# A fused decoder layer: the rounds of scores in the cross-attention stage are set apart, each between halves or thirds of full-height products

## The chip, the cores and the metric

One NeuronCore of a Trainium2 chip runs the whole program in one launch. The metric is the device time of one execution in microseconds (us). The engines named below are TensorE (PE, with its weight loads shown as PEld), VectorE (DVE), ScalarE (ACT), GpSimd (POOL) and the DMA queue of SyncE (SP). Each runs its own list of instructions in order, and waits on semaphores.

## The reference

Input x is 4 x 1024 x 512 in fp32, the context 4 x 2048 x 384. Three sublayers follow each other, each with a residual and a layer norm: linear attention, a cross sublayer, and a feed-forward with quantized weights and activations. Only the cross sublayer matters here. Cut to that:

```
Q = (x_text @ Wq).reshape(Bb, Tt, H, DH)                 # H = 4 heads, DH = 32
scores = einsum('bthd,bghd->bhtg', Q, K) / sqrt(DH)      # 2048 keys
topv, topi = top_k(scores, 32)
probs = softmax(topv)
attn_mean = zeros.at[..., topi].set(probs).mean(axis=1)
c_t = attn_mean @ V
x = layernorm(x_text) * (1 + gate * scale_in(c_t)) + gate * shift_in(c_t)
y = s4d(x)                                               # a long convolution, by FFT
y = y * (1 + gate * scale_out(c_t)) + gate * shift_out(c_t)
h = gelu(layernorm(x_text + y) @ W1 + b1) @ W2 + b2
```

## The kernel before, in words

The program runs its stages one after the other: `a_` (linear attention), `p_` (preparation of keys, film weights and convolution kernel), `c_` (cross, the function `cross`), and `f_` (feed-forward). The change is in `cross` alone.

`cross` works in 32 tiles of 128 tokens (`t`), eight per batch element, with four heads each; head number `j = 4 t + h`. The work of a head goes through all engines:
- PE makes the scores: `queries(t)` turns the tile x (transposes) and projects q. `scores(t, p)` makes those of the head pair `p`: four rounds of 512 keys, each round one product of 32 rows for each of the two heads, and one of a single row that adds the mask. The result lies in PSUM, `p_s`, with one bank per head of the pair, so that a round waits for ACT to have copied the last one.
- ACT copies the scores to SBUF (`copy_s`, the ring `s` of five rows).
- DVE finds the top 32 of 2048 in four scans (MAX8 and MATCH_REPLACE8, lines 1490 to 1498). In the middle of a head's scans stands the reciprocal of the previous head's softmax sum (`invert`, line 1483).
- ACT's `below(j)` marks what is under the 32nd value and sums the exponentials; POOL's `cut(j)` subtracts the marks; ACT's `weigh(j)` takes the exponential, and `diagonal(j)` makes a diagonal of the reciprocal.
- PE's `attn(j)` multiplies the weights by this diagonal and so turns them: 16 products of 128 x 128 (the turning products), summed over four heads in `p_a`. `copy_a` moves them to SBUF.

Once per tile PE makes `context` (48 products with the values), `film` in two parts (twice two accumulations of 512 columns), and what belongs to the convolution: `spectra` (the forward products, 64 columns each) and `slot` (tiles 0 to 7 transpose the convolution's kernel, tiles 11 and on make the inverse products). `context`, `film`, `queries`, `spectra` and `slot` share the two PSUM banks `p_m`, so each waits for ACT to copy the one before it (`copy_q`, `copy_f`, `copy_u`, `copy_slot`, `copy_fi`, `copy_fo`). POOL makes the convolution's small transforms: `transform` behind `copy_f`, from tile 10 on also `convolved` and `finished`, between the cuts; and `modulate` applies the first film part and stores the tile.

The order on each engine is written out by hand, as one loop over tiles per engine; nothing reorders it. In a step `t` of that loop PE does `attn` of the last two heads of tile t-1 and the first two of tile t, the scores of pair 1 of tile t in one block of four rounds, and those of pair 0 of tile t+1 in another. SP loads x, the normalized x, keys and values of the next batch, and spectra, in its own loop with its waits.

One product in fp32 is two instructions on PE, so 16 turning products are 32 in the trace, and 48 are 96. The names `c_p_s`, `c_p_a`, `c_p_m`, `c_s` in the profile are the tiles `p_s`, `p_a`, `p_m`, `s` of the code.

Of the kernel before, what the change touches and what calls it, by code (L numbers as in the profile page):

```python
# [8 lines left out]
ACT = mybir.ActivationFunctionType  # L9
# [5 lines left out]
P = 128  # L15
B, S, D = 4, 1024, 512
TOK = B * S
CH = S // P
# [436 lines left out]
N2, DV, NH2 = 2048, 384, 4  # L455
# [433 lines left out]
def cross(nc, x1, xn, keysT, values, film_w, film_b, mask_row, text_mask, Wq, eye, xm, mod_out, conv_k, D_skip, dft, idft,  # L889
# [4 lines left out]
    with ExitStack() as ctx:  # L894
# [106 lines left out]
        def forwards(t):  # L1001
            return sum(forward_job(i) is not None for i in range(t + 1))
# [142 lines left out]
        def _(pe):  # L1145
# [1 line left out]
            pe.wait_ge(core_in, 16 * 3)  # L1147
            pe.wait_ge(consts, 2)

            def queries(t):  # L1150
# [4 lines left out]
                last.then_inc(xT_done, 1)  # L1155
                pe.wait_ge(xT_copied, t + 1)
                for k in range(KD):
                    last = mm(p_m[:, 1, 0:P], wq[:, k, :], xT[:, k * P:(k + 1) * P], start=(k == 0), stop=(k == KD - 1))
                last.then_inc(q_done, 1)

            def scores(t, p):
                pe.wait_ge(q_copied, t + 1)
                pe.wait_ge(keys_in, 80 * (t // CH + 1))
                for c in range(4):
                    cols = slice(c * 512, (c + 1) * 512)
                    for i in range(2):
                        r = HS * (2 * p + i)
                        at_least(pe, s_copied, (t * 2 + p) * 8 + 2 * c + i - 1)
                        mm(p_s[:, i, :], qT[r:r + HS, t % 2, :], kt[r:r + HS, cols], start=True, stop=False)  # L1169
                        mm(p_s[:, i, :], oneb[r:r + 1, :], mrow[r:r + 1, cols], start=False, stop=True).then_inc(s_done, 1)  # L1170

            def attn(j):
                t, h = j // NH2, j % NH2
                if h == 0:
                    at_least(pe, aT_copied, t)
                pe.wait_ge(diag_ready, j + 1)
                pe.wait_ge(w_ready, j + 1)
                for n in range(GB):
                    last = mm(p_a[:, n, :], s[:, j % RING, n * P:(n + 1) * P], diag[:, j % 2, :],  # L1179
                              start=(h == 0 and n % 4 == 0), stop=(h == NH2 - 1 and n % 4 == 3),  # L1180
                              skip_group_check=True)
                last.then_inc(attn_done, 1)

            def spectra(t):

# [37 lines left out]
            def context(t):  # L1223
                at_least(pe, f_copied, forwards(t + 1))
                pe.wait_ge(values_in, 16 * (t // CH + 1))
                pe.wait_ge(aT_copied, t + 1)
                if t + 2 < TILES:
                    pe.wait_ge(xT_copied, t + 3)
                for k in range(KV3):
                    for n in range(GB):  # L1230
                        last = mm(p_m[:, 0, k * P:(k + 1) * P], vals[:, n, k * P:(k + 1) * P], aT[:, n, :],  # L1231
                                  start=(k == 0 and n == 0), stop=(k == KV3 - 1 and n == GB - 1),
                                  skip_group_check=True)
                last.then_inc(uT_done, 1)

            def film(t, part):
                if part == 0:
# [12 lines left out]
                    last = mm(p_m[:, n, :], oneb[0:BR, :], fb[:, c * D:(c + 1) * D], start=False, stop=True)  # L1250
                last.then_inc(fo_done if part else fi_done, 1)

            queries(0)
            scores(0, 0)
# [23 lines left out]
            attn(LAST - 1)  # L1278
            attn(LAST)
            slot(TILES)  # L1280
            context(TILES - 1)
            film(TILES - 1, 0)

            def rest_forward(i):
# [34 lines left out]
        def _(act):  # L1319
            a = nc.scalar.activation  # L1320

            def copy_q(t):
                act.wait_ge(xT_done, t + 1)
                at_least(act, q_done, t)
                a(xT[:], p_m[:, 0, :], ACT.Copy).then_inc(xT_copied, 1)
                act.wait_ge(q_done, t + 1)
                a(qT[:, t % 2, :], p_m[:, 1, 0:P], ACT.Copy).then_inc(q_copied, 1)

            def copy_s(t, p, part):
                at_least(act, attn_done, (t - 1) * NH2 + 2 * p + 1)  # L1330
                for c in range(2 * part, 2 * part + 2):
                    for i in range(2):
                        act.wait_ge(s_done, (t * 2 + p) * 8 + 2 * c + i + 1)
                        a(s[:, (t * NH2 + 2 * p + i) % RING, c * 512:(c + 1) * 512], p_s[:, i, :], ACT.Copy).then_inc(s_copied, 1)  # L1334

            def below(j):

# [52 lines left out]
            def copy_slot(t):  # L1390
# [5 lines left out]
                else:  # L1396
                    at_least(act, y_out, 16 * (g - NCB))
                    a(yb[:].rearrange("p n c -> p (n c)"), p_m[:, 1, :], ACT.Copy).then_inc(slot_copied, 1)  # L1398

            copy_q(0)  # L1400
            copy_s(0, 0, 0)
            copy_s(0, 0, 1)
            for t in range(TILES):
                j = t * NH2
                if t:
                    below(j - 1)
                if t > 1:
                    copy_fo(t - 2)
                copy_s(t, 1, 0)
                if t:  # L1410
                    weigh(j - 1)
                    diagonal(j - 1)
                copy_s(t, 1, 1)
                if t + 1 < TILES:
                    copy_q(t + 1)
# [6 lines left out]
                weigh(j)  # L1422
                diagonal(j)

                below(j + 1)
                if t:
                    copy_u(t - 1)
                if t + 1 < TILES:
                    copy_s(t + 1, 0, 0)
                weigh(j + 1)  # L1430
                diagonal(j + 1)
                if t + 1 < TILES:
                    copy_s(t + 1, 0, 1)
                if slot_job(t) is not None:
                    copy_slot(t)

                below(j + 2)
                if t:
                    copy_fi(t - 1)
                weigh(j + 2)  # L1440
                diagonal(j + 2)
            below(LAST)
            weigh(LAST)
            diagonal(LAST)
            copy_fo(TILES - 2)
# [101 lines left out]
        def _(pool):  # L1547
# [69 lines left out]
            for t in range(TILES):  # L1617
                job = forward_job(t)
                masked_identity(t)
                j = t * NH2  # L1620
                if t:
                    cut(j - 1)
                if t > 1:
                    store_mod(t - 2)
# [7 lines left out]
                if t:  # L1632
# [5 lines left out]
            cut(LAST)  # L1638
            store_mod(TILES - 2)
            modulate(TILES - 1)  # L1640
            store_mod(TILES - 1)
# [770 lines left out]
```

## Time and profile before

| | us |
|---|---|
| three runs | 5045.29, 5044.64, 5043.18 |
| median | 5044.64 |
| profiled execution | 5042.79 |
| its span | 5040.9 |
| PE busy | 4416.3 (88%) |
| DVE busy | 3805.5 (75%) |
| POOL busy | 2186.9 (43%) |
| ACT busy | 2068.8 (41%) |

The span is the time from the first to the last instruction of the profiled execution; 1.9 us lie around it. The cross stage is from about 978 us (the first scan of DVE) to some 3530 us. "Busy" of PE counts pipelined matmuls with modelled ends. PEclk is TensorE's granted clock, 1.00 for 2.4 GHz and 0.50 for 1.2 GHz. In the page's 40 slices it reads 9 and more in the first stages, and 7 to 8 in the cross stage.

### The profile page before, as it was taken

The numbers are of one execution on the slowest core, as the hardware profiler recorded it, in microseconds if no ns is written. First come the engines' busy times: TensorE is split into PE (matmuls) and PEld (weight loads), VectorE is DVE, ScalarE is ACT, GpSimd is POOL, SyncE is SP. The second block draws the span as 40 slices with busy tenths as digits, with TensorE's granted clock in tenths as the row PEclk, the third lists the DMA queues.
The fourth block names the chain that finished last, engine by engine and source line by source line (L and its number), as shares of the span: only waits on it lengthen the run. The fifth ranks groups of instructions, "written<-read, shape, count | busy, mean of one in ns | idle before, by whom it ended". The sixth has DMA issues, their size and how long they took to land. (4 is left out here: it accounts for less than half of the span.)

```text
span 5040.9 us, 70529 instructions
## 1 busy us (share of the span) xinstructions
PE 4416.3 (88%) x28066; PEld 3194.9 (63%) x28066; DVE 3805.5 (75%) x4097; ACT 2068.8 (41%) x3816; POOL 2186.9 (43%) x2260
## 2 busy tenths in 40 slices
PE   8999977589999999999999999987579989898984
PEld 6777753356665676676766667667456666666662
DVE  5666659699999988888788887876256767777667
ACT  3433322144444444444444444431234545444453
POOL 1111116435454566766667666670233333333321
PEclk9999988678888877777777777788789999999996
DMA  2111115300011001111011110023531211111101
GB/s 84 51 46 50 49 48 185 118 24 28 24 42 61 26 28 34 38 53 36 28 32 38 54 37 26 30 69 76 193 104 43 61 44 58 47 58 54 51 26 36
DMA packets 214587, 275.98 MB, mean 55 GB/s; under 512 B 96659, under 2 KB 144403, under 8 KB 210224
## 3 DMA queue, kind: packets, MB, share of 16 engines
q1 hardware_dynamic: 196850, 216.91, 14.2%
q0 software_dynamic: 17408, 54.56, 2.9%
q8 instruction: 222, 3.64, 0.3%
q14 instruction: 107, 0.88, 0.1%
HBM read 186.44 MB, written 84.98 MB: 54 GB/s over the span
## 5 line engine op out<-in xcount | busy, mean ns | idle before, releaser
L1555 POOL TENSOR_TENSOR c_s<-c_s,c_z 128x2048 f32<-128x2048 f32 x128 | 580.5, 4535 | 792.8 <-ACT c_z L1344 790.8
L1875 PE MATMUL f_p_g<-f_hT,f_w 128*128 128x128 f32 x4096 | 538.3, 295 | 69.8 <-ACT f_gT L1975 55.4
L1496 DVE MAX8 c_top<-c_z 128x8 f32<-128x2048 f32 x256 | 585.0, 2285 | 4.7 <-issue 0.2
L1875 PEld LDWEIGHTS f_p_g<-f_hT,f_w 128*128 128x128 f32 x4096 | 526.7, 211 | 90.4 <-ACT f_gT L1975 58.2
L1497 DVE MATCH_REPLACE8 c_z<-c_top,c_z 128x2048 f32<-128x2048 f32 x256 | 582.6, 2276 | 0.0
L1169 PE MATMUL c_p_s<-c_kt,c_qT 32*128 32x512 f32 x1024 | 500.9, 864 | 87.1 <-ACT c_s L1334 85.8
L1179 PEld LDWEIGHTS c_p_a<-c_diag,c_s 128*128 128x128 f32 x4096 | 528.2, 211 | 49.5 <-ACT c_diag L1358 25.8
L1179 PE MATMUL c_p_a<-c_diag,c_s 128*128 128x128 f32 x4096 | 531.3, 293 | 25.2 <-ACT c_diag L1358 25.2
L1883 PE MATMUL f_p_o<-f_w,f_gT 128*128 128x512 f32 x1024 | 481.8, 592 | 0.0
L1334 ACT ACTIVATE c_s<-c_p_s 128x512 f32<-128x512 f32 x512 | 278.2, 594 | 455.0 <-PE c_p_s L1170 454.6
L1249 PE MATMUL c_p_m<-c_wf,c_uT 128*128 128x512 f32 x768 | 415.7, 684 | 22.6 <-ACT c_yb L1398 16.3
L1231 PE MATMUL c_p_m<-c_aT,c_vals 128*128 128x128 f32 x3072 | 393.3, 296 | 38.1 <-ACT c_fz L1388 33.4
L1231 PEld LDWEIGHTS c_p_m<-c_aT,c_vals 128*128 128x128 f32 x3072 | 387.3, 211 | 42.5 <-ACT c_fz L1388 37.5
L1169 PEld LDWEIGHTS c_p_s<-c_kt,c_qT 32*128 32x128 f32 x1024 | 173.7, 233 | 294.7 <-ACT c_s L1334 283.9
L1249 PEld LDWEIGHTS c_p_m<-c_wf,c_uT 128*128 128x128 f32 x768 | 164.4, 222 | 213.8 <-issue 211.7
L1498 DVE MAX8 c_top<-c_z 128x8 f32<-128x2048 f32 x128 | 293.8, 2295 | 4.4
L1490 DVE MAX8 c_top<-c_s 128x8 f32<-128x2048 f32 x128 | 293.8, 2295 | 4.4
L1491 DVE MATCH_REPLACE8 c_z<-c_top,c_s 128x2048 f32<-128x2048 f32 x128 | 291.3, 2276 | 0.0
L2124 DVE TENSOR_TENSOR f_hs<-f_p_c,f_rs 128x257 f32<-128x257 f32 (+1 forms) x256 | 108.6, 424 | 232.1 <-PE f_p_c L1894 230.6
L1352 ACT ACTIVATE c_s<-c_s,c_nb 128x2048 f32<-128x2048 f32 x128 | 255.2, 1994 | 27.9 <-POOL c_s L1555 27.9
L1344 ACT ACTIVATE c_z<-c_s,c_tb 128x2048 f32<-128x2048 f32 x128 | 256.3, 2002 | 0.0
L1883 PEld LDWEIGHTS f_p_o<-f_w,f_gT 128*128 128x128 f32 x1024 | 174.5, 190 | 123.8 <-issue 115.8
(362 smaller groups left out, 8103.4 us busy)
## 6 DMA issues: line engine op xcount, KB each, us to landing
mod_out<-c_fo POOLq DMA_DIRECT2D x32, 512.0 KB, 3.0
f_mr<-mod_out SPq DMA_DIRECT2D x32, 512.0 KB, 4.8
p_ct<-in_ctxT SPq DMA_DIRECT2D x16, 768.0 KB, 5.1
c_vals<-in_ctx SPq DMA_DIRECT2D x4, 3072.0 KB, 12.0
c_kb<-kspec SPq DMA_DIRECT2D x22, 512.0 KB, 3.3
a_xt<-in_xT SPq DMA_DIRECT2D x32, 256.0 KB, 3.1
a_xr<-in_x SPq DMA_DIRECT2D x32, 256.0 KB, 2.6
x<-a_out POOLq DMA_DIRECT2D x32, 256.0 KB, 2.5
```

The costliest lines, as they stand in the source:

```text
L1169: mm(p_s[:, i, :], qT[r:r + HS, t % 2, :], kt[r:r + HS, cols], start=True, stop=False)
L1179: last = mm(p_a[:, n, :], s[:, j % RING, n * P:(n + 1) * P], diag[:, j % 2, :], start=(h == 0 and n % 4 == 0), stop=(h == NH2 - 1 and n % ...
L1231: last = mm(p_m[:, 0, k * P:(k + 1) * P], vals[:, n, k * P:(k + 1) * P], aT[:, n, :], start=(k == 0 and n == 0), stop=(k == KV3 - 1 and n ...
L1249: mm(p_m[:, n, :], uT[:, k, :], wf[:, k, c * D:(c + 1) * D], start=(k == 0), stop=False)
L1490: st.link(v.max(best[0], row))
L1491: st.link(v.match_replace(work, best[0], row, NEG))
L1496: st.link(v.max(best[n], work))
L1497: st.link(v.match_replace(work, best[n], work, NEG))
L1498: v.max(best[3], work).then_inc(z_done, 1)
L1555: pool.tensor_tensor(row, row, low, ALU.subtract).then_inc(cut_ready, 1)
L1875: last = mm(p_g[:, f % 8, :], w1[:, k, f * P:(f + 1) * P], hT[:, k * P:(k + 1) * P], start=(k == 0 and f % 4 == 0), stop=(k == KD - 1 and ...
L1883: last = mm(p_o[:], gT[:, f, :], w2[:, f, :], start=(f == 0), stop=(f == FT - 1))
```

## The change

`scores` makes one round per call, `queries` is divided in `turn` (transposes) and `queries` (projection), `attn` in two halves of 8 products, `context` in its three accumulations. PE's loop then puts single rounds between them. The second part of `film` moves to the next step, and with it `copy_fi`, `copy_fo` and POOL's `modulate`. ACT's loop copies one round at a time, on both sides of `weigh` and `diagonal`, and copies the slot's result behind `weigh` of the third head. The instructions themselves are as they were; after the last tile the two halves of `attn` and one part of `film` follow.

```diff
-            def scores(t, p):
+            def scores(t, p, c):
                 pe.wait_ge(q_copied, t + 1)
                 pe.wait_ge(keys_in, 80 * (t // CH + 1))
-                for c in range(4):
-                    cols = slice(c * 512, (c + 1) * 512)
-                    for i in range(2):
+                cols = slice(c * 512, (c + 1) * 512)
+                for i in range(2):
...
-            def attn(j):
+            def attn(j, part):
                 t, h = j // NH2, j % NH2
-                if h == 0:
-                    at_least(pe, aT_copied, t)
-                pe.wait_ge(diag_ready, j + 1)
-                pe.wait_ge(w_ready, j + 1)
-                for n in range(GB):
+                if part == 0:
+                    if h == 0:
+                        at_least(pe, aT_copied, t)
+                    pe.wait_ge(diag_ready, j + 1)
+                    pe.wait_ge(w_ready, j + 1)
+                for n in range(8 * part, 8 * part + 8):
...
                 if t:
-                    attn(j - 2)
-                scores(t, 1)
+                    attn(j - 2, 0)
+                scores(t, 1, 0)
+                if t:
+                    attn(j - 2, 1)
+                if t > 1:
+                    film(t - 2, 1)
+                scores(t, 1, 1)
+                if t + 1 < TILES:
+                    turn(t + 1)
+
+                if t:
+                    attn(j - 1, 0)
+                scores(t, 1, 2)
+                if t:
+                    attn(j - 1, 1)
                 if t + 1 < TILES:
                     queries(t + 1)
-                if t:
-                    attn(j - 1)
                 if forward_job(t) is not None:
                     spectra(t)
+                scores(t, 1, 3)
                 if t:
-                    context(t - 1)
-                attn(j)
+                    context(t - 1, 0)
+
+                attn(j, 0)
                 if t + 1 < TILES:
-                    scores(t + 1, 0)
+                    scores(t + 1, 0, 0)
+                attn(j, 1)
+                if t:
+                    context(t - 1, 1)
+                if t + 1 < TILES:
+                    scores(t + 1, 0, 1)
+                if t:
+                    context(t - 1, 2)
+
+                attn(j + 1, 0)
+                if t + 1 < TILES:
+                    scores(t + 1, 0, 2)
+                attn(j + 1, 1)
                 if slot_job(t) is not None:
                     slot(t)
+                if t + 1 < TILES:
+                    scores(t + 1, 0, 3)
                 if t:
                     film(t - 1, 0)
-                attn(j + 1)
-                if t:
-                    film(t - 1, 1)
...
                 below(j)
                 if t:
                     copy_a(t - 1)
+                copy_s(t, 1, 2)
+                if t + 1 < TILES:
+                    copy_q(t + 1)
+                weigh(j)
+                diagonal(j)
                 if forward_job(t) is not None:
                     copy_f(t)
...
             for t in range(TILES):
                 job = forward_job(t)
                 if t:
                     cut(j - 1)
                 if t > 1:
+                    modulate(t - 2)
+                cut(j)
+                if t > 1:
                     store_mod(t - 2)
-                cut(j)
...
                 cut(j + 2)
-                if t:
-                    modulate(t - 1)
```

PE in a step from tile 11 on, before: from the end of the block for pair 1 (1154 transposes, 1158 q, 1179 turning products, 1199 forward products, 1231 context) to the start of the next block.

```order
L1154 MATMUL c_p_m<-c_ident,c_xt 128x128 x4
L1158 MATMUL c_p_m<-c_xT,c_wq 128x128 x4
L1179 MATMUL c_p_a<-c_diag,c_s 128x128 x16
L1199 MATMUL c_p_m<-c_cx,c_fm 128x64 x16
L1231 MATMUL c_p_m<-c_aT,c_vals 128x128 x48
L1179 MATMUL c_p_a<-c_diag,c_s 128x128 x16
L1169 MATMUL c_p_s<-c_kt,c_qT 128x512
L1170 MATMUL c_p_s<-c_mrow,c_oneb 128x512
```

The same place in the changed kernel (1181 turning products, 1170 and 1171 a round, 1160 q, 1202 forward products):

```order
L1154 MATMUL c_p_m<-c_ident,c_xt 128x128 x4
L1181 MATMUL c_p_a<-c_diag,c_s 128x128 x8
L1170 MATMUL c_p_s<-c_kt,c_qT 128x512
L1171 MATMUL c_p_s<-c_mrow,c_oneb 128x512
L1170 MATMUL c_p_s<-c_kt,c_qT 128x512
L1171 MATMUL c_p_s<-c_mrow,c_oneb 128x512
L1181 MATMUL c_p_a<-c_diag,c_s 128x128 x8
L1160 MATMUL c_p_m<-c_xT,c_wq 128x128 x4
L1202 MATMUL c_p_m<-c_cx,c_fm 128x64 x16
L1170 MATMUL c_p_s<-c_kt,c_qT 128x512
```

The projection of q moved behind a head's turning products, and a round stands inside these; the next round stands behind the forward products.

ACT around the copy of the slot product, before (1334 scores, 1398 slot copy, 1340 to 1346 `below(j+2)`, 1373 copy_fi, 1352 `weigh`, 1358 `diagonal`):

```order
L1334 ACTIVATE c_s<-c_p_s 128x512 x4
L1398 ACTIVATE c_yb<-c_p_m 128x512
L1340 ACTIVATE c_tb<-c_top 128x1
L1341 ACTIVATE c_nb<-c_top 128x1
L1344 ACTIVATE c_z<-c_s,c_tb 128x2048
L1346 ACTIVATE c_topx,c_den<-c_top,c_nb 128x32
L1373 ACTIVATE c_fi<-c_p_m 128x1024
L1352 ACTIVATE c_s<-c_s,c_nb 128x2048
L1358 ACTIVATE c_diag<-c_identm,c_rd 128x128
```

The same head in the changed kernel (1376 to 1382 `below`, 1370 scores, 1388 `weigh`, 1434 slot copy, 1394 `diagonal`):

```order
L1376 ACTIVATE c_tb<-c_top 128x1
L1377 ACTIVATE c_nb<-c_top 128x1
L1380 ACTIVATE c_z<-c_s,c_tb 128x2048
L1382 ACTIVATE c_topx,c_den<-c_top,c_nb 128x32
L1370 ACTIVATE c_s<-c_p_s 128x512 x2
L1388 ACTIVATE c_s<-c_s,c_nb 128x2048
L1434 ACTIVATE c_yb<-c_p_m 128x512
L1394 ACTIVATE c_diag<-c_identm,c_rd 128x128
L1370 ACTIVATE c_s<-c_p_s 128x512 x2
```

The slot copy moved from ahead of `below` to behind `weigh` of the same head, and copy_fi left this head.

## Rows read from the trace of the kernel before

**Rows 1.** List of waits, whole span: engine, line, released by: us in total, times, longest.

```profile
DVE c_rd L1483 <- issue: 282.0, 54, 10.6
```

**Rows 2.** DVE in order of time: start, us, line, instruction, idle time before it.

```profile
1110.62 2.29 DVE L1490 MAX8 c_top<-c_s 128x8 f32<-128x2048 f32 x1
...
1744.70 2.29 DVE L1490 MAX8 c_top<-c_s 128x8 f32<-128x2048 f32 x1
...
2404.93 2.29 DVE L1490 MAX8 c_top<-c_s 128x8 f32<-128x2048 f32 x1
...
2421.47 2.29 DVE L1490 MAX8 c_top<-c_s 128x8 f32<-128x2048 f32 x1
...
2441.39 0.16 DVE L1483 RECIPROCAL c_rd<-c_den 128x1 f32<-128x1 f32 x1 [10.52 <-issue]
...
2448.49 2.29 DVE L1490 MAX8 c_top<-c_s 128x8 f32<-128x2048 f32 x1
...
2476.33 0.16 DVE L1483 RECIPROCAL c_rd<-c_den 128x1 f32<-128x1 f32 x1 [1.89 <-issue]
```

**Rows 3.** Windows: stretch, us, busy of PE, PEld, DVE, ACT, POOL, granted clock, DMA.

```profile
2400.26:2478.77 78.51, 73.58 (x379) 54.07 (x377) 65.21 (x45) 33.91 (x53) 52.00 (x60) 0.78 0.10 31
2421.70:2425.60 3.90, 2.97 (x12) 1.00 (x9) 3.87 (x3) 2.25 (x5) 3.90 (x2) 1.00 0.00 0
2425.80:2442.60 16.80, 15.80 (x48) 10.07 (x46) 6.21 (x6) 6.98 (x12) 9.52 (x11) 0.50 0.15 47
2480.40:2483.60 3.20, 2.09 (x19) 1.95 (x19) 3.13 (x3) 1.56 (x3) 0.38 (x2) 1.00 0.00 0
```

**Rows 4.** PE in order of time, one step from tile 11 on.

```profile
2400.06 3.68 PE L1199 MATMUL c_p_m<-c_cx,c_fm 128*128 128x64 f32 x32
2404.86 12.61 PE L1231 MATMUL c_p_m<-c_aT,c_vals 128*128 128x128 f32 x96 [1.11 <-ACT c_fz L1388]
2417.31 3.74 PE L1179 MATMUL c_p_a<-c_diag,c_s 128*128 128x128 f32 x32
2420.97 1.13 PE L1169 MATMUL c_p_s<-c_kt,c_qT 32*128 32x512 f32 x4
...
2423.06 1.18 PE L1169 MATMUL c_p_s<-c_kt,c_qT 32*128 32x512 f32 x3 [0.73 <-ACT c_s L1334]
...
2431.15 7.09 PE L1219 MATMUL c_p_m<-c_fv,c_gm 128*128 128x64 f32 x32
2439.01 4.66 PE L1249 MATMUL c_p_m<-c_wf,c_uT 128*128 128x512 f32 x6 [0.78 <-ACT c_yb L1398]
...
2450.09 2.74 PE L1249 MATMUL c_p_m<-c_wf,c_uT 128*128 128x512 f32 x6
```

**Rows 5.** ACT in order of time, the same step.

```profile
2400.26 1.88 ACT L1363 ACTIVATE c_aT<-c_p_a 128x2048 f32<-128x2048 f32 x1 [2.53 <-PE c_p_a L1179]
2403.78 1.02 ACT L1388 ACTIVATE c_fz<-c_p_m 128x1024 f32<-128x1024 f32 x1 [1.64 <-PE c_p_m L1199]
...
2425.41 1.99 ACT L1352 ACTIVATE c_s<-c_s,c_nb 128x2048 f32<-128x2048 f32 x1
...
2427.60 1.07 ACT L1334 ACTIVATE c_s<-c_p_s 128x512 f32<-128x512 f32 x2
...
2438.27 0.60 ACT L1398 ACTIVATE c_yb<-c_p_m 128x512 f32<-128x512 f32 x1 [6.42 <-PE c_p_m L1219]
...
2438.99 2.00 ACT L1344 ACTIVATE c_z<-c_s,c_tb 128x2048 f32<-128x2048 f32 x1
```

**Rows 6.** POOL in order of time: transform, cut, first and last of convolution.

```profile
2404.88 1.28 POOL L827 TENSOR_TENSOR c_fw<-c_fz 128x512 f32<-128x512 f32 x1 [2.82 <-ACT c_fz L1388]
...
2416.53 4.55 POOL L1555 TENSOR_TENSOR c_s<-c_s,c_z 128x2048 f32<-128x2048 f32 x1
2421.03 2.37 POOL L1601 TENSOR_TENSOR c_fz<-c_fw,c_kb 128x1024 f32<-128x1024 f32 x1
...
2433.33 0.73 POOL L864 TENSOR_TENSOR c_ft<-c_fz 128x256 f32<-128x256 f32 x1
```

More of the change, by code:

```diff
@@ L1148, in _, with turn @@
             pe.wait_ge(consts, 2)
-            def queries(t):
+            def turn(t):
                 pe.wait_ge(x_in[t % 2], 16 * (t // 2 + 1))
@@ L1155, in queries @@
                 last.then_inc(xT_done, 1)
+            def queries(t):
                 pe.wait_ge(xT_copied, t + 1)
@@ L1181, in attn @@
                               skip_group_check=True)
-                last.then_inc(attn_done, 1)
+                if part:
+                    last.then_inc(attn_done, 1)
             def spectra(t):
@@ L1221, in slot, with context @@
                 last.then_inc(slot_done, 1)
[L1223 to L1234, printed above, removed]
+            def context(t, k):
+                if k == 0:
+                    at_least(pe, f_copied, forwards(t + 1))
+                    pe.wait_ge(values_in, 16 * (t // CH + 1))
+                    pe.wait_ge(aT_copied, t + 1)
+                    if t + 2 < TILES:
+                        pe.wait_ge(xT_copied, t + 3)
+                for n in range(GB):
+                    last = mm(p_m[:, 0, k * P:(k + 1) * P], vals[:, n, k * P:(k + 1) * P], aT[:, n, :],
+                              start=(k == 0 and n == 0), stop=(k == KV3 - 1 and n == GB - 1),
+                              skip_group_check=True)
+                if k == KV3 - 1:
+                    last.then_inc(uT_done, 1)
             def film(t, part):
@@ L1251, in film @@
                 last.then_inc(fo_done if part else fi_done, 1)
+            turn(0)
             queries(0)
-            scores(0, 0)
+            for c in range(4):
+                scores(0, 0, c)
             for t in range(TILES):
@@ L1320, in _, with copy_x @@
             a = nc.scalar.activation
-            def copy_q(t):
+            def copy_x(t):
                 act.wait_ge(xT_done, t + 1)
@@ L1325, in copy_q, with copy_s @@
                 a(xT[:], p_m[:, 0, :], ACT.Copy).then_inc(xT_copied, 1)
+            def copy_q(t):
                 act.wait_ge(q_done, t + 1)
                 a(qT[:, t % 2, :], p_m[:, 1, 0:P], ACT.Copy).then_inc(q_copied, 1)
-            def copy_s(t, p, part):
+            def copy_s(t, p, c):
                 at_least(act, attn_done, (t - 1) * NH2 + 2 * p + 1)
[L1331 to L1334, printed above, removed]
+                for i in range(2):
+                    act.wait_ge(s_done, (t * 2 + p) * 8 + 2 * c + i + 1)
+                    a(s[:, (t * NH2 + 2 * p + i) % RING, c * 512:(c + 1) * 512], p_s[:, i, :], ACT.Copy).then_inc(s_copied, 1)
             def below(j):
@@ L1398, in copy_slot @@
                     a(yb[:].rearrange("p n c -> p (n c)"), p_m[:, 1, :], ACT.Copy).then_inc(slot_copied, 1)
+            copy_x(0)
             copy_q(0)
-            copy_s(0, 0, 0)
-            copy_s(0, 0, 1)
+            for c in range(4):
+                copy_s(0, 0, c)
             for t in range(TILES):
@@ L1407, in _ @@
                 if t > 1:
-                    copy_fo(t - 2)
+                    copy_fi(t - 2)
                 copy_s(t, 1, 0)
@@ L1412, in _ @@
                     diagonal(j - 1)
+                if t > 1:
+                    copy_fo(t - 2)
                 copy_s(t, 1, 1)
                 if t + 1 < TILES:
-                    copy_q(t + 1)
+                    copy_x(t + 1)
                 below(j)
@@ L1419, in _ @@
                     copy_a(t - 1)
+                copy_s(t, 1, 2)
[3 more added lines that the diff above has]
+                diagonal(j)
                 if forward_job(t) is not None:
                     copy_f(t)
-                weigh(j)
-                diagonal(j)
+                copy_s(t, 1, 3)
                 below(j + 1)
-                if t:
-                    copy_u(t - 1)
                 if t + 1 < TILES:
@@ L1433, in _ @@
                     copy_s(t + 1, 0, 1)
+                if t:
+                    copy_u(t - 1)
+                below(j + 2)
+                if t + 1 < TILES:
+                    copy_s(t + 1, 0, 2)
+                weigh(j + 2)
                 if slot_job(t) is not None:
                     copy_slot(t)
[L1437 to L1440, printed above, removed]
                 diagonal(j + 2)
+                if t + 1 < TILES:
+                    copy_s(t + 1, 0, 3)
             below(LAST)
+            copy_fi(TILES - 2)
             weigh(LAST)
@@ L1631, in _ @@
                 cut(j + 2)
-                if t:
-                    modulate(t - 1)
                 if job is not None and not of_kernel(job):
@@ L1638, in _ @@
             cut(LAST)
+            modulate(TILES - 2)
             store_mod(TILES - 2)
```

19 lines of the change are left out of this document (12 added, 7 removed).

## Prediction, made before the changed kernel was run

> **What bounds the kernel now.** I read the list of waits first, for the engine with the steadiest work in the cross stage: VectorE (DVE), which scans four heads per tile. It is to be seen there that its idle time in the stage is one entry, 282.0 us in 54 waits ahead of the reciprocal c_rd [rows 1]. Then DVE's rows in order of time, for where these waits stand. An undisturbed head takes 16.54 us, from 2404.93 to 2421.47, so a tile cannot take less than 66.2 us. In a late tile the head that begins at 2421.47 has a wait of 10.52 us in its middle, and two heads later there is one of 1.89 us [rows 2]; 66.2 + 12.4 = 78.6, and from one copy of p_a to the same copy a tile later it is 78.51 us [rows 3]. The nine tiles from 1110.62 to 1744.70 took 634.1 us, 38.6 more than 9 x 66.16 [rows 2]. The remaining 282 - 39 = 243 us lie in the 20 tiles after them, the last of 32 apart. These two numbers, 39 and 243, are all that an order of work can give back.
>
> Why the 10.52 us? The reciprocal waits for the sum that ScalarE (ACT) makes in `below`. Head j+2 was scanned at 2421.47, but `below(j+2)` has its large instruction at 2438.99, because ACT stood 6.42 us at copy_slot ahead of it [rows 5], which waits for TensorE's (PE's) slot product, which stands behind four rounds of scores [rows 4]. So PE is late, and what makes it late is its clock as much as its work. PE is busy 73.58 us of a tile at a mean granted clock of 0.78 [rows 3]. As only 1.0 and 0.5 (2.4 and 1.2 GHz) appear, it was at half for (1 - 0.78) x 2 x 78.51 = 34.5 us, which cost 17 us of work: at full rate PE would be busy for some 57 us, less than DVE's 66.2.
>
> What precedes a fall is in the windows. From 2421.7 to 2425.6 PE did only score products (32 rows high), 2.97 us busy of 3.90, at full clock; the next 16.80 us are at half. Another fall is short: the end of the 64-column forward products and a wait, 2.09 us busy of 3.20 at full, half behind it [rows 3]. Eight rounds per tile in two blocks of four are thus where most of the half-clock time comes from (the block, and the slot product and half a film behind it). A round costs 1.36 us at full clock (2420.97 to 2423.06 less the wait of 0.73), and in a block PE then waits for ACT's two copies of 1.07 us [rows 4, 5].
>
> **The change, part by part.** Each round now stands between products of full height: a head's turning products (3.74 us) are cut in two halves around a round, context in thirds. The instructions are the same; no DMA is added. PE gains two things: the copies of a round run beside other products (each round's period of about 2.0 us falls to 1.36: 8 x 0.65, less where it waited at half clock, about 4 us), and between a round and the next there are at least 1.9 us of full-height work, so that the block that preceded the fall is gone. I take the clock as full there. No row shows such a mixture; the nearest, half a tile of pure products, is at full clock, and pure rounds lose it, so the bounds are "full everywhere" and "half everywhere".
>
> What the change adds is coupling. ACT copies the slot result only behind `weigh(j+2)`, and the first film product waits for that copy; the film's second half moves a slot later, behind copy_fi; the forward products wait for q_copied, now behind copy_a and a copied round. POOL has its transform and its convolution between the cuts as before, but now `cut(j+2)` holds the film. That closes a loop over one tile, and I add it up. T is when DVE starts a tile's first head, directly after ACT's last copy of its scores; the slot copy is 1.6 us before T (what ACT does behind it: diagonal and the round, from the rows weigh to copy, 2.2 - 1.9 + 1.1, with handoffs).
> - film, first half: two accumulations of 2.74 us, 5.6 at full. PE has been idle before it (below), so it begins at half clock as at 2439.01, where the first took 4.66: + 1.9. Ends T + 5.9.
> - turning product and one round 3.7 + 1.4; film, second half 5.6; a round and the transpose 2.0; turning product and a round 5.1: T + 23.7 [rows 4].
> - ACT: copy_a 1.88, a round 1.07, q 0.3: T + 27.0 [rows 5].
> - forward products 3.68 at full; 7.1 at half, as the slot product of the same shape took [rows 4]; copy_f 1.02: T + 31.7 or T + 35.1.
> - POOL: from 2404.88 transform, cut and convolution to 2434.06 are 29.2, and the next cut is 4.5: + 33.7 [rows 6]: T + 65.4 or T + 68.8.
> - ACT: weigh and diagonal 2.2, slot copy 0.5, round 1.1 [rows 5]: T + 69.2 or 72.6, and a dozen handoffs at 0.1 (copy_f ends at 2404.80, POOL starts at 2404.88): 70.4 or 73.8.
>
> So a late tile is bound by this loop, not by DVE. Between the two values I take 72.5: PE has 2.4 us without work ahead of the forward products (q projection over, q not yet copied), like the wait of 1.1 in front of context behind which the clock fell, and loses the clock somewhere in them. PE idles then 5 us or more ahead of the film. DVE will stand some 5 us at two heads' starts together, for c_s, not at c_rd.
>
> Late tiles: 243 - 20 x (72.5 - 66.2) = 117 us saved. Of the nine early tiles only the last has a convolution (and the one before it no forward job): without its 13 us POOL's loop has slack, and it counts whether the tile's second pair of heads has its scores in time. q is copied 5.8 us behind a head's end (`below` 2.5, from the end of the copy at 2438.87 to DVE's start at 2441.39; copy_a 1.9; a round 1.1; q 0.3), forward products 3.7 to 7.1, a round 1.4 to 2.9, and the copies of both (2), in sum 12.9 to 17.8 against 16.5. I leave 0.5 us for each and 2 for the ninth, 6 of the 39 us: 33 saved. The first two tiles have no wait and keep none. Three times the keys of the next batch are loaded behind the last round of the old ones, and that round now stands closer to the first of the new: a context third (12.61 / 3 = 4.2) and half a product (1.9) are between, 6 us. No row here prices this; bounds are 0 and 4 us for each of three loads, I take 0. The film half that moves behind the last tile lies beside the last head's cut (ACT and POOL then take over 9 us): 0, bounds 0 and 3. Sum: 5042.8 - 150 = 4893 for the profiled execution; the median shown is 1.9 above it, so 4895.
>
> **The rule that speaks against it.** The Trainium skill, "TensorE: Matmul & The Clock Gate", section "Why this matters for your kernels", asks that there be no long idle gap between bursts of matmuls, since one returns the clock to half rate; it says nothing of matmuls that fill only a quarter of the array's rows. By it alone, the score blocks would not cost clock, and the new idle stretches of 2.4 and 5 us would: the sum would have no clock gain and come near the slower rival below. The trace bears out more than the rule: in front of the fall at 2425.8 PE had one wait of 0.73 us for a copy and was else at work [rows 3, 4].
>
> **Rivals.**
> - Smaller gain: forward products, the round behind them and the first context third all at half, a round more at half in the film's slot: 73.8 + 1.5 or so, 75.3 per late tile. 243 - 182 + 20 = 81 saved: 4964. For it: a 64-column product behind a wait already lost the clock once.
> - Larger gain: forward products and film keep the full clock: 70.4 - 1.9 = 68.5. 243 - 46 + 36 = 233 saved: 4812. Against it: the idle time ahead of both. The end of this side is DVE unhindered everywhere, 4763.
> - Slower: the loop's PE part (27 us at full) runs mostly at half clock, since PE now waits at three places in the loop and a round stands in each stretch. The loop reaches today's 78.5 when 12 us of work at half clock are added to those I took (they cost 6). With the first film wholly at half (3.7 more), the first turning product and round (5) and the second film (5.6) it is 72.5 + 14.3 = 86.8: 20 x 8 = 160 slower, and the early gain gone, 5205. Against it: in the rows the film regains the full clock before it ends (the second of its two accumulations, like that at 2450.09, takes 2.74).
> - No change: the late tile stays at 78.5 by another wait (a DMA of x or xn, now asked for one slot later). Nothing in the rows is near; 5044.
>
> **How the numbers follow.** Forecast (70.4 to 74 per late tile, 4860 to 4930) 0.45, smaller gain (up to 4990) 0.27, larger gain 0.13, none 0.04, slower 0.11. Faster by over 0.2% (about what a measurement of this kernel can tell from no change) 0.85, within it 0.04, slower 0.11. The range goes from the middle of the larger gain, 4825, to the end of the smaller, 4990.
>
> **What would show it.** Right: late tiles of 71 to 74 us with DVE's waits at c_s (the MAX8 on c_s) instead of c_rd; no half clock between turning products and rounds; mean granted clock of a tile near 0.85; PE idle over 4 us ahead of the first film product, released by c_yb's copy; POOL's gap between the convolution and the cut of head j+2 gone. Wrong: half clock across several halves of turning products, which means that one round is enough to lose it; POOL's cut not being late; or late tiles at 66 us, which breaks the loop.

## The result

| | before | changed |
|---|---|---|
| median, us (4 runs each) | 5044.97 | 4898.96 |
| lowest and highest | 5043.18, 5045.51 | 4896.70, 4902.59 |
| profiled execution, its span | 5042.79, 5040.9 | 4900.3, 4898.4 |

The ratio is 0.9712, 95% interval 0.9695 to 0.9729: 2.9% faster. The forecast was 4895 us, a ratio of 0.970.

### The profile page after: what moved, and what is told of

It is laid out like the page before. It is cut to its first block and busy times, and to the rows that moved or that the text cites. A ratio compares the mean times of both kernels' runs of the same rounds, so it can differ in the third digit from the quotient of the medians.

```text
span 4898.4 us, 70845 instructions
## 1 busy us (share of the span) xinstructions
PE 4201.7 (86%) x28066; PEld 3061.9 (63%) x28066; DVE 3798.7 (78%) x4097; ACT 2061.7 (42%) x3816; POOL 2187.6 (45%) x2260
## 5 line engine op out<-in xcount | busy, mean ns | idle before, releaser
L1923 PE MATMUL f_p_g<-f_hT,f_w 128*128 128x128 f32 x4096 | 539.4, 295 | 67.4 <-ACT f_gT L2023 53.0
L1181 PEld LDWEIGHTS c_p_a<-c_diag,c_s 128*128 128x128 f32 x4096 | 489.2, 195 | 119.0 <-issue 90.7
L1253 PE MATMUL c_p_m<-c_wf,c_uT 128*128 128x512 f32 x768 | 420.0, 690 | 142.2 <-ACT c_yb L1434 120.6
L1234 PEld LDWEIGHTS c_p_m<-c_aT,c_vals 128*128 128x128 f32 x3072 | 420.8, 224 | 61.7 <-issue 59.7
L1234 PE MATMUL c_p_m<-c_aT,c_vals 128*128 128x128 f32 x3072 | 435.1, 310 | 3.8 <-ACT c_aT L1399 2.5
L1537 DVE MAX8 c_top<-c_s 128x8 f32<-128x2048 f32 x128 | 293.8, 2295 | 139.2 <-ACT c_s L1370 136.4
L1170 PE MATMUL c_p_s<-c_kt,c_qT 32*128 32x512 f32 x1024 | 333.7, 720 | 20.1 <-ACT c_s L1370 19.8
L1202 PE MATMUL c_p_m<-c_cx,c_fm 128*128 128x64 f32 x960 | 185.2, 383 | 70.5 <-ACT c_qT L1364 70.5
```

The source lines that it names most:

```text
L1253: mm(p_m[:, n, :], uT[:, k, :], wf[:, k, c * D:(c + 1) * D], start=(k == 0), stop=False)
L1537: st.link(v.max(best[0], row))
L1923: last = mm(p_g[:, f % 8, :], w1[:, k, f * P:(f + 1) * P], hT[:, k * P:(k + 1) * P], start=(k == 0 and f % 4 == 0), stop=(k == KD - 1 and ...
```

## The profile after

The waits of DVE first, in the list of waits of the changed kernel (us in total, times, longest). Line 1537 is the MAX8 on c_s, a head's first scan; 1253 is film, 1202 the forward products.

```profile
DVE c_top L1537 <- ACT c_s L1370: 136.4, 48, 5.8
PE c_p_m L1253 <- ACT c_yb L1434: 120.6, 21, 9.0
PE c_p_m L1202 <- ACT c_qT L1364: 70.5, 29, 4.5
```

The wait of film for the slot copy was there before, but short:

```profile
PE c_p_m L1249 <- ACT c_yb L1398: 16.3, 21, 0.8
```

The 282.0 us at c_rd [rows 1] are gone as an entry, and 136.4 us have come at the heads' starts: DVE now waits for scores. PE's wait for the slot copy has grown from 16.3 to 120.6 us, and its wait for q is new. Then DVE in order of time: the tile that starts at 1723.14 (tile 11) is the first of the 20 late ones, those in which the convolution's inverse products are made, and 2369.34, 2440.13 and 2513.72 are three tile starts in a row, to hold against [rows 2].

```profile
1112.46 2.29 DVE L1537 MAX8 c_top<-c_s 128x8 f32<-128x2048 f32 x1
...
1723.14 2.30 DVE L1537 MAX8 c_top<-c_s 128x8 f32<-128x2048 f32 x1 [1.43 <-ACT c_s L1370]
...
2369.34 2.29 DVE L1537 MAX8 c_top<-c_s 128x8 f32<-128x2048 f32 x1 [2.10 <-ACT c_s L1370]
...
2404.96 2.30 DVE L1537 MAX8 c_top<-c_s 128x8 f32<-128x2048 f32 x1 [2.57 <-ACT c_s L1370]
...
2440.13 2.29 DVE L1537 MAX8 c_top<-c_s 128x8 f32<-128x2048 f32 x1 [2.12 <-ACT c_s L1370]
...
2513.72 2.29 DVE L1537 MAX8 c_top<-c_s 128x8 f32<-128x2048 f32 x1 [2.09 <-ACT c_s L1370]
```

The nine early tiles take 610.7 us from 1112.46 to 1723.14, 15 over 9 x 66.16 (39 before). A late tile takes about 70.8 us (nine of the twenty) or 73.6 to 74.0 us (ten), not strictly in turn, and the mean over twenty is 72.1. The windows of two such tiles, and of two stretches inside (busy of PE, PEld, DVE, ACT, POOL, granted clock, DMA), answer to [rows 3]:

```profile
2369.34:2440.13 70.79, 63.29 (x377) 46.79 (x377) 65.21 (x44) 33.59 (x53) 51.98 (x60) 0.89 0.11 34
2440.13:2513.72 73.59, 65.20 (x377) 48.33 (x377) 65.21 (x44) 33.59 (x54) 51.96 (x60) 0.85 0.10 33
2378.00:2395.00 17.00, 16.28 (x92) 10.10 (x88) 16.76 (x12) 9.87 (x14) 5.58 (x4) 1.00 0.23 63
2468.70:2480.00 11.30, 11.30 (x48) 9.40 (x49) 5.87 (x3) 4.77 (x8) 3.89 (x6) 0.50 0.09 37
```

From 2378 to 2395 PE does turning products, three rounds, film, transposes and the projection, all at full clock. PE's idle time in a tile has not gone down: it was 4.9 us (78.51 less 73.58) and is now 7.5 and 8.4. What has gone down is its busy time for the same instructions, from 73.6 to 63.3 and 65.2 us. The stretch at half is the forward products, the round behind them and the start of context. PE in order of time shows where the two tiles differ, to hold against [rows 4]:

```profile
2368.13 4.69 PE L1253 MATMUL c_p_m<-c_wf,c_uT 128*128 128x512 f32 x6 [5.59 <-ACT c_yb L1434]
...
2378.83 2.05 PE L1181 MATMUL c_p_a<-c_diag,c_s 128*128 128x128 f32 x16
...
2393.22 1.06 PE L1160 MATMUL c_p_m<-c_xT,c_wq 128*128 128x128 f32 x8
2396.59 4.67 PE L1202 MATMUL c_p_m<-c_cx,c_fm 128*128 128x64 f32 x32 [2.31 <-ACT c_qT L1364]
...
2467.82 7.06 PE L1202 MATMUL c_p_m<-c_cx,c_fm 128*128 128x64 f32 x32 [2.31 <-ACT c_qT L1364]
```

The forward products take 4.67 us in one tile and 7.06 in the next: behind the wait of 2.31 us the clock falls in their midst or ahead of them, which is 2.4 of the 2.8 us between the two tiles. On ACT the slot copy, behind POOL's late cut and `weigh`, starts at 2438.20, 1.9 us ahead of the next tile's start. On POOL the gap between the convolution and this cut is gone, as forecast:

```profile
2430.93 0.73 POOL L864 TENSOR_TENSOR c_ft<-c_fz 128x256 f32<-128x256 f32 x1
2431.74 4.53 POOL L1602 TENSOR_TENSOR c_s<-c_s,c_z 128x2048 f32<-128x2048 f32 x1
```

## The experiments

All are compared with the kernel before on the same chip. "Late tile" is the mean distance of the starts of tiles 11 to 31 (before 78.4, changed 72.1), "early tile" that of tiles 2 to 11 (70.5 and 67.9), read from DVE's rows; DVE's own time is 66.2. In e4, e8 and e10 the scores are other numbers, since those products sum over all four heads; sizes and counts are the same.

| kernel | median us | ratio (95%) | early tile | late tile |
|---|---|---|---|---|
| e1 slot copy first | 4786.69 | 0.9478 (0.9463 to 0.9492) | 66.2 | 67.4 |
| e2 q copy first | 4801.04 | 0.9508 (0.9494 to 0.9523) | 66.2 | 68.1 |
| e3 both | 4755.63 | 0.9418 (0.9402 to 0.9433) | 66.2 | 66.2 |
| e4 before, full height | 4890.19 | 0.9684 (0.9670 to 0.9699) | 68.4 | 71.7 |
| e5 before, below first | 5068.15 | 1.0050 (1.0035 to 1.0065) | 72.7 | 78.0 |
| e6 whole turning products | 4805.95 | 0.9524 (0.9508 to 0.9539) | 66.3 | 68.3 |
| e7 rounds in pairs | 5038.82 | 0.9991 (0.9977 to 1.0005) | 70.6 | 77.5 |
| e8 changed, full height | 4983.69 | 0.9879 (0.9865 to 0.9894) | 70.8 | 74.8 |
| e9 whole and slot first | 4786.17 | 0.9478 (0.9464 to 0.9493) | 66.3 | 67.6 |
| e10 before, both edits | 4915.37 | 0.9732 (0.9715 to 0.9748) | 71.2 | 71.5 |

**Is it the height of the products that takes the clock?** e4 is the kernel before with one line changed.

```diff
-                        mm(p_s[:, i, :], qT[r:r + HS, t % 2, :], kt[r:r + HS, cols], start=True, stop=False)
+                        mm(p_s[:, i, :], qT[:, t % 2, :], kt[:, cols], start=True, stop=False)
```

> The kernel before, order untouched, with the score products over all 128 rows instead of the head's 32 (this sums over the four heads, so the scores are other numbers; sizes and counts are the same). It asks whether the height of the products or idle time takes PE's clock. A round takes 4 x 0.43 + 2 x 0.21 = 2.1 us at full clock instead of 1.36 and a wait of 0.66, so no time is gained by itself. Theory (the blocks of low products lose the clock): the two long half-clock stretches of a late tile go, the mean granted clock of a late tile goes from 0.78 to 0.95 or so, the tile from 78.5 to 66.2 to 69 us; 4780 to 4850. Rival (idle gaps alone lose it, height is nothing): clock 0.78 and 5040 to 5100, since the rounds no longer overlap.

The window of one late tile of e4, and the first round of a block, where the two heads no longer overlap:

```profile
2379.21:2450.39 71.18, 67.39 (x377) 44.78 (x376) 65.22 (x44) 34.57 (x52) 51.99 (x60) 1.00 0.11 34
```
```profile
2388.13 1.02 PE L1169 MATMUL c_p_s<-c_kt,c_qT 128*128 128x512 f32 x2
2389.08 0.39 PE L1170 MATMUL c_p_s<-c_mrow,c_oneb 1*128 1x512 bf16 x1
2389.40 1.12 PE L1169 MATMUL c_p_s<-c_kt,c_qT 128*128 128x512 f32 x2
2390.46 0.38 PE L1170 MATMUL c_p_s<-c_mrow,c_oneb 1*128 1x512 bf16 x1
2390.77 1.12 PE L1169 MATMUL c_p_s<-c_kt,c_qT 128*128 128x512 f32 x2
```

The clock is 1.00 over the whole tile, where it was 0.78 with the same order. From 1800 to 3100 us it is 0.99 in the mean, 0.78 before:

```profile
1800.00:3100.00 1300.00, 1231.76 (x6816) 821.35 (x6815) 1183.42 (x799) 628.12 (x944) 944.73 (x1075) 0.99 0.13 41
```
A round costs 2.6 us (2388.13 to 2390.77), twice as much as with low products, and the tile is still 7 us shorter. The longer rounds also fill most of the waits for the copies, so two things changed at once. In the kernel before, PE was busy for 15.80 of 16.80 us, mostly in low and 64-column products, and stayed at half all the same [rows 3], so it is not idle time that kept it there. What let it fall is not parted by this run: it can be the height of the products or the short waits between them (0.73 and 0.20 us ahead of the fall), and low rounds in a row without a wait were not run. The time is above my 4780 to 4850, since I had summed a round as 2.1 us: PE is busy for 67.4 of 71.2 us, which leaves little room for waits.

**Is it enough that ACT is unblocked?** e5 moves one call in the kernel before.

```diff
-                if slot_job(t) is not None:
-                    copy_slot(t)
-
                 below(j + 2)
+                if slot_job(t) is not None:
+                    copy_slot(t)
```

> The kernel before, with one move on ACT: below(j+2) ahead of the copy of the slot product, so that DVE's reciprocal, which had the 10.52 us wait, no longer waits behind PE's slot product. Theory (PE with its half-clock stretches is what bounds a late tile: 73.6 us busy and 5 waiting): the wait moves to another place of DVE, the late tile stays at 77 to 78.5, 5015 to 5050. Rival (the gain of the change is this unblocking of ACT, not the clock or the rounds): late tiles at 68 to 72, 4830 to 4910.

```profile
2390.73:2469.23 78.50, 73.56 (x377) 54.08 (x376) 65.21 (x44) 33.92 (x52) 52.03 (x59) 0.78 0.10 31
```

The same clock, the same PE time, the same 78.5. DVE's 12.4 us of waits in a tile (10.52 and 1.89) are 12.4 us again, ahead of the reciprocals of three heads:

```profile
2401.69 0.16 DVE L1483 RECIPROCAL c_rd<-c_den 128x1 f32<-128x1 f32 x1 [1.56 <-issue]
2425.58 0.17 DVE L1483 RECIPROCAL c_rd<-c_den 128x1 f32<-128x1 f32 x1 [7.38 <-issue]
2462.13 0.16 DVE L1483 RECIPROCAL c_rd<-c_den 128x1 f32<-128x1 f32 x1 [3.50 <-issue]
```

The kernel is 0.5% slower, outside my 5015 to 5050, mostly because the early tiles went from 70.5 to 72.7. The wait that the profile named was not the one to remove. e10 adds e5's edit to e4, to see whether ACT's order counts once the clock is full.

> The kernel before with both edits: score products over all 128 rows (other scores, same sizes) and below(j+2) ahead of the slot copy. Alone, the first took a late tile from 78.5 to 71.2 us with a DVE wait of 5 us at the reciprocal left, the second left it at 78.5. Theory (half clock bounds first, ACT's order second): together 66.2 to 68 us per late tile, 4760 to 4810. Rival (the 5 us are PE's work, since the full-height rounds are longer, and only change their place): 70 to 71.5, 4870 to 4900.

The rival was right on the tile: 71.5 us per late tile. The time, 4915, is above its range and 25 us above e4, as the early tiles went from 68.4 to 71.2. At full clock, too, this swap on ACT gives nothing; PE is busy for 66.4 of 70.0 us from 2350 to 2420, at a clock of 0.98.

**How many rounds may stand together?** e7 puts the changed kernel's rounds in pairs, e6 leaves them single but no longer cuts a head's turning products. Shown is one of the four places of each, on PE.

```diff
# e7
                     scores(t + 1, 0, 2)
+                    scores(t + 1, 0, 3)
                 attn(j + 1, 1)
# e6
                 attn(j, 0)
+                attn(j, 1)
                 if t + 1 < TILES:
                     scores(t + 1, 0, 0)
-                attn(j, 1)
```

> The changed kernel with the rounds in four pairs instead of eight single ones (two behind the turning products of heads j-2 and j, two between the halves of heads j-1 and j+1), their copies on ACT in pairs as well. PE then waits 0.66 us inside each pair, 2.6 us per tile. Theory (the clock falls behind a stretch of low products, and two rounds with the wait between are 3.4 us of it, about what stood ahead of the fall in the kernel before): some pairs lose the clock, the mean granted clock of a late tile falls below the changed kernel's 0.85 to 0.89, and late tiles take 75 to 79 us: 4955 to 5040. Rival (only blocks of four lose it): the waits alone, late tiles 72 to 74: 4900 to 4935.

> The changed kernel with a head's turning products in one piece: each single round stands behind the 16 products instead of between two halves of 8. Theory (it is enough that rounds stand singly): no fall of the clock is added, the late tiles stay at 70.7 to 73.7, 4885 to 4915. Rival (the halves matter, since without them a round stands next to a copy wait, a transpose or the forward products): half clock behind some rounds and late tiles of 75 us or more, 4950 and up.

e7 gives all of the gain back, as forecast (77.5 us per late tile, 5039). PE at one of its pairs:

```profile
2395.49 1.13 PE L1170 MATMUL c_p_s<-c_kt,c_qT 32*128 32x512 f32 x4
2396.45 0.39 PE L1171 MATMUL c_p_s<-c_mrow,c_oneb 1*128 1x512 bf16 x2
2397.66 1.52 PE L1170 MATMUL c_p_s<-c_kt,c_qT 32*128 32x512 f32 x4 [0.83 <-ACT c_s L1367]
2398.59 0.80 PE L1171 MATMUL c_p_s<-c_mrow,c_oneb 1*128 1x512 bf16 x2
2399.33 3.67 PE L1181 MATMUL c_p_a<-c_diag,c_s 128*128 128x128 f32 x16
```

The second round ends slower (0.80 instead of 0.39) and the eight turning products behind it take 3.67 us instead of 1.95: the clock fell in the pair. This is the rule and not one case: of the eight turning products that stand directly behind a round, from 1120 to 3160 us and where the trace has all their records, 110 of 111 take 2.05 us in the changed kernel, and 46 of 51 take 3.4 to 3.8 us in e7, where they stand behind a pair. Here are three tiles of e7, and an idle stretch of PE ahead of film in the changed kernel:

```profile
2360.04:2438.85 78.81, 71.07 (x374) 50.99 (x374) 65.22 (x45) 34.36 (x52) 50.36 (x59) 0.82 0.10 31
2438.85:2517.53 78.68, 68.45 (x377) 48.57 (x377) 65.20 (x44) 34.27 (x52) 51.88 (x60) 0.87 0.10 31
2206.38:2282.25 75.87, 65.88 (x365) 48.09 (x364) 65.21 (x44) 34.25 (x52) 51.56 (x60) 0.87 0.13 41
```
```profile
2362.60:2368.10 5.50, 0.00 (x0) 0.00 (x0) 4.60 (x3) 2.60 (x3) 5.41 (x8) 0.73 0.00 0
```

The mean clock of 0.82 to 0.87 is hardly less than the 0.85 and 0.89 above. But in the changed kernel part of the half clock lies where PE is idle, while in e7 more of it falls on work: PE is busy for 68.5 us in the mean of these three tiles instead of 64.2. The wait of 0.83 us in each pair is 3.3 us per tile beside that, and part of the loss.

e6 missed both forecasts: it is faster than the changed kernel by 93 us (4805.95 against 4898.96). PE at the place of the wait for q:

```profile
2276.51 3.74 PE L1181 MATMUL c_p_a<-c_diag,c_s 128*128 128x128 f32 x32
2280.17 1.13 PE L1170 MATMUL c_p_s<-c_kt,c_qT 32*128 32x512 f32 x4
2281.14 0.39 PE L1171 MATMUL c_p_s<-c_mrow,c_oneb 1*128 1x512 bf16 x2
2281.45 1.16 PE L1160 MATMUL c_p_m<-c_xT,c_wq 128*128 128x128 f32 x8
2283.45 3.76 PE L1202 MATMUL c_p_m<-c_cx,c_fm 128*128 128x64 f32 x32 [0.84 <-ACT c_qT L1362]
```

With whole products `p_a` is complete one round (1.4 us) earlier, so ACT copies it beside the round. The wait for q falls from 2.31 to 0.84, and the forward products keep the full clock (3.76). That is 1.5 us of wait and 0.9 to 3.3 of half clock (3.76 against 4.67 and 7.06), all of it in the loop: 68.3 instead of 72.1. The halves bought no clock; they cost 3.8 us a tile.

**Does a single round cost clock?** e8 is e4's line in the changed kernel.

> The changed kernel with score products over all 128 rows (they sum over the four heads, so the scores are other numbers). A round takes 2.7 us at full clock instead of 1.36 and no longer overlaps its two heads, as the rounds of the full-height run of the kernel before show. Theory (a single round between full-height products costs no clock, what is left of half clock comes from PE's two waits): the mean clock of a late tile rises only because PE has less to wait, and no more than 3 us of half clock go; five rounds of the loop cost 1.4 each, late tiles 76 to 80 and 4980 to 5060, slower than the changed kernel. Rival (single rounds still cost clock): the time stays or falls, 4850 to 4900, at a clock of 0.95 and more.

```profile
2348.46:2426.43 77.97, 75.66 (x377) 49.98 (x377) 65.21 (x45) 34.24 (x54) 51.36 (x58) 0.88 0.10 31
2426.43:2498.62 72.19, 67.30 (x377) 44.92 (x376) 65.21 (x45) 34.08 (x54) 52.45 (x62) 0.99 0.10 33
```

The kernel is 1.7% slower than the changed one, and 4984 is in the range of the theory; the late tile, 74.8 us in the mean, is below its 76 to 80. The wait for q is 2.31 us in every late tile. Behind it the forward products take 7.06 us in one tile and 3.76 in the next, in turn, where in the changed kernel they take 4.6 to 7.1 in every late tile that has all its records. So more half clock went than the 3 us I allowed, and beside a wait the height of the rounds, or their length, does count. Between full-height products low rounds cost no clock: the stretch 2378 to 2395 above is at 1.00.

**Is a late tile the loop that I summed?** e1 takes film out of it, e2 the wait for q, e3 both. All are in ACT's loop.

```diff
# e1
-                weigh(j + 2)
                 if slot_job(t) is not None:
                     copy_slot(t)
+                weigh(j + 2)
# e2
-                if t:
-                    copy_a(t - 1)
                 copy_s(t, 1, 2)
                 if t + 1 < TILES:
                     copy_q(t + 1)
+                if t:
+                    copy_a(t - 1)
```

> The changed kernel, with the copy of the slot product on ACT ahead of weigh of head j+2 instead of behind it. Theory (the late tiles, mean 72.1 us, are a loop: film waits for the slot copy, this for POOL's cut, this for the convolution): film starts some 4 to 5 us earlier, as soon as the slot product and its round are done, and falls out of the loop. What is left is bound by when a head ends: the q copy cannot come before T + 22.4, forward products at half clock to T + 29.5, copy 1.0, POOL 33.7, ACT 4: 68.5 to 69.5 us per late tile, so 20 x 3 = 60 us less than 4899: 4840 (4820 to 4865). Early tiles stay at 68.2. Rival (the cut is late but PE is bound by its own work, so an earlier film only moves its idle time): no change, 4890 to 4905.

> The changed kernel, with the copy of q (and of the round before it) on ACT ahead of the copy of p_a. Theory: the forward products no longer wait 2.3 us for q, lie directly behind the projection, and so keep the full clock (3.7 us instead of 4.7 to 7.1). The loop of a late tile loses 2.0 us of wait and 1 to 3.4 us of half clock: 68 to 68.7 us instead of 70.7 and 73.7 in turn; early tiles 66.2 to 66.6 instead of 68.2. 20 x 3.8 + 8 x 1.7 = 90 less: 4810 (4795 to 4830). Rival (the clock falls in the forward products whatever is ahead of them, since they are 64 columns): only the 2 us of wait, 40 to 45 less: 4855.

> Both orders of ACT together (slot copy ahead of weigh, q copy ahead of the copy of p_a). Theory: no loop is longer than DVE's 66.2 us, and DVE runs without waits but for the start: 136 us of waits at c_s go, 4763 (4755 to 4785). Rival (something else, such as POOL's sum or PE's work at a clock that falls elsewhere, comes next): late tiles at 68 us or more, 4800.

e2 came as summed: 68.1 per late tile, the early ones 66.2, 4801. In its trace the forward products wait 0.46 us for q and take 3.76:

```profile
2412.63 3.76 PE L1202 MATMUL c_p_m<-c_cx,c_fm 128*128 128x64 f32 x32 [0.46 <-ACT c_qT L1364]
```

e1 gave 112 us instead of 60. In its trace film stands directly behind a round, and the wait has moved to the forward products of the same tile:

```profile
2338.52 7.00 PE L1202 MATMUL c_p_m<-c_cx,c_fm 128*128 128x64 f32 x32 [4.42 <-ACT c_qT L1364]
...
2375.94 1.13 PE L1170 MATMUL c_p_s<-c_kt,c_qT 32*128 32x512 f32 x4
2376.91 0.39 PE L1171 MATMUL c_p_s<-c_mrow,c_oneb 1*128 1x512 bf16 x2
2377.22 2.84 PE L1253 MATMUL c_p_m<-c_wf,c_uT 128*128 128x512 f32 x6
```

Film starts without a wait and at full clock (2.84 against 4.69), but this gives nothing here, since PE then waits 4.42 us for q. The sum had the right path and missed two sizes (T is again the start of a tile on DVE). The late tiles came out at 67.4 instead of 69: in the tile that starts at 2316.39 the copy of q ends at T + 22.0 instead of T + 22.4, the forward products end at T + 29.1 instead of 29.5, ACT takes 3.4 us instead of 4 from the end of the last cut to the next tile, and the handoffs take less than the half to one microsecond that I allowed. Over twenty tiles that is some 33 us. The early tiles fell to 66.2 as well, 14 us that I had not counted: their 2 us were on the same path from film to the forward products. e3 is the fastest, at the low end of its forecast: the window of a late tile is DVE's own 66.2 us.

```profile
2368.97:2435.14 66.17, 62.67 (x384) 46.69 (x384) 65.21 (x44) 33.93 (x53) 52.89 (x62) 0.92 0.12 37
```

No tile of e3 takes more than 66.2 us, and PE still runs at 0.92: its forward products wait 2.7 us for q and take 4.7 to 7.1 us in nearly all late tiles, but they end by T + 27.4, which is early enough that no tile grows longer. e9 was to reach the same with whole products.

> The changed kernel with the turning products in one piece and the slot copy ahead of weigh. Theory (what is left of the loop with whole products is film's wait of 7.8 us for the slot copy, released by POOL's late cut): that wait goes, no loop is longer than DVE's 66.2 us, 4750 to 4765, as with both ACT orders in the changed kernel. Rival (the slot and film products stand so that the clock falls again, or the whole products delay a round that DVE needs): late tiles of 67 us or more, 4775 and up.

It did not, and the rival was right: 67.6 and 4786, like e1. With film gone from the loop PE comes earlier to the q copy and waits for it, and the forward products run at half:

```profile
2340.17 7.06 PE L1202 MATMUL c_p_m<-c_cx,c_fm 128*128 128x64 f32 x32 [3.82 <-ACT c_qT L1362]
```

In e1 and in e9 the copy of q ends at T + 22.0, behind `below`, copy_a and a round on ACT; with e2's order added (e3) it ends at T + 20.2. Once film is out of the loop, whole products give nothing more, and only e2's order brings q earlier.

## Why the prediction was right, and where it was not

- The sum of 150 us against 142.5 measured (5042.8 less 4900.3): close in part by luck. The late tiles gave 8 us more than forecast and the early ones 10 less, tile 2 starts 1.8 us later than before, and behind the start of tile 31 the kernel takes 4.1 us longer.
- What bounds the kernel before: held. The 39 and 243 us can be given back: in e3 no tile takes more than 66.2 us, and from tile 2 to tile 31 it is 282.6 us shorter than before. It takes 6 us less behind tile 31 too, so that the two numbers were not quite all that an order can give.
- The clock's part: held, and is the main gain. PE is busy 8 to 10 us less in a tile with the same instructions, while its idle time has grown: the waits inside the rounds are nearly gone (85.8 us in the whole run before, 19.8 now), but more has come ahead of film and of the forward products. That the blocks of rounds take the clock is shown by e4 (1.00 at full height) and e7 (pairs lose it); whether their height alone does it, or height together with the short waits in a block, stays open, since both runs changed both. The Trainium skill ("TensorE: Matmul & The Clock Gate", section "Why this matters for your kernels") names idle gaps alone as what takes the clock, and longer ones than the wait for q; here the forward products fell behind 2.31 us of wait, and kept the full clock behind 0.46 (e2) and 0.84 (e6), but in e4, with high products and PE's waits of up to 1.11 us left in, none cost clock.
- The loop: held closely. Forecast were 70.4 and 73.8 us by the clock of the forward products, measured are 70.8 and 73.6; q copied at T + 27.0, measured T + 27.1; PE's waits 2.4 and 5, measured 2.31 and 5.19 to 5.59; film's first part 4.66, measured 4.69; DVE's waits moved to c_s, 4.7 and 7.4 us per tile (I had said 5). The mean is 72.1 instead of 72.5, 125 us saved instead of 117. e1 and e2 each break the loop where it was said to pass.
- The early tiles: mis-sized. Forecast were 6 us left, measured 15 (67.9 per tile). The sum took q's copy as bound by the head's end, 22.3 us behind the tile's start, while it came behind PE's film, turning products and rounds: in the tile that starts at 1452.89 it ends at 1477.31, 24.4 us behind. e1 shows it, since moving the slot copy alone frees these tiles.
- "The clock is full between the halves": true, but the halves were not its cause. That cutting the turning products delays `p_a`, and with it the copy that q waits behind, stood in my own sum (turning product and a round, 5.1, ahead of copy_a) and I did not read it as a cost. e6 prices it at 3.8 us per late tile.
- The key loads and the moved film: taken as 0. The tiles with a key load, 7, 15 and 23, take 68.3, 73.6 and 70.8 us, as their neighbours do; no cost can be seen. From the last scan to the last film product it is 61.1 us, 58.4 before: 2.7 us, inside the bounds of 0 and 3 but not 0. No run shows how much of it is the moved film.

## What to carry to other kernels

Look at what stands together on TensorE, not only at whether it is busy: low products in a block can take its clock, and it is enough to part them with high ones; test it by making them high for one run, though the results are then other numbers. Here that held for blocks with short waits inside; blocks without them were not run. When work is interleaved, follow every copy on the engine that empties PSUM: its order, not the product's, closed the loop here, and two swaps there were worth as much again as the whole change (4899 to 4756). The longest wait in the profile is not by itself a place to gain: in e5 its cause was moved away, and the same 12.4 us came back at three places.

## What was not expected of the hardware

- The clock stayed at 1.00 over a whole tile, and at 0.99 in the mean from 1800 to 3100 us, with four rounds in a row once the products were 128 rows high (e4), and through PE's single waits of up to 1.11 us there.
- Two low rounds with a wait of 0.83 us between them lost it in 46 of 51 places (e7); one low round in front of turning products kept it in 110 of 111 (the changed kernel).
- The same wait of 2.31 us ahead of the forward products cost them clock in all 18 late tiles of the changed kernel that have all their records (4.6 to 7.1 us against 3.76), but only in every other one with high rounds (e8: 7.06 and 3.76 in turn).
- Two heads' low products on different rows overlap: a round takes 1.36 us low and 2.6 us high, for the same count of columns.
